# First half's input projection and convolution as one TensorE product, second half's softplus and B/C parts off VectorE, the memsets ahead of them

## The reference, cut to what matters

```
x  = einsum('ed,bld->bel', in_proj_w, hidden)         # input projection
xc = conv over l, 4 taps per channel, causal          # xp padded by 3
u  = silu(xc + conv_b)
dt_lo, B, C = split(einsum('ke,bel->bkl', x_proj_w, u))   # 8, 16, 16 rows
delta = softplus(einsum('er,brl->bel', dt_proj_w, dt_lo) + dt_proj_b)
A = -exp(A_log)
step: state = state * exp(delta * A) + (delta * u) * B ;  y = sum_n state * C
y = (y + D * u) * silu(z)                              # z: layer norm of x
```

## Time and profile before

| | us |
|---|---|
| median of 3 runs (lowest, highest) | 882.12 (879.97, 882.24) |
| the profiled execution, its own time | 880.29 |
| its span, first to last instruction | 878.5 |
| busy in the span: PE, DVE, ACT, POOL | 785.6, 572.9, 451.5, 424.5 |

### The profile page before, as it was taken

The page is one execution under the profiler, slowest core; times in us unless marked ns, Lnnn a source line. Parts: engine busy times, 40 slices in busy tenths (PEclk is TensorE's granted clock), DMA queues, the critical chain, the costliest instruction groups (busy, mean ns, idle before and its releaser), DMA issues. The chain is left out here.

```text
span 878.5 us, 13771 instructions
## 1 busy us (share of the span) xinstructions
PE 785.6 (89%) x4691; PEld 659.1 (75%) x4694; DVE 572.9 (65%) x948; ACT 451.5 (51%) x911; POOL 424.5 (48%) x325
## 2 busy tenths in 40 slices
PE   7366576699999996999999999999979999999997
PEld 2122222378888885999999999999858888888886
DVE  7999999845333345888888888888766433333333
ACT  4433344273343334777777777777634343433432
POOL 1464666136565645435344353443224565655653
PEclk9686999899999999999999999999979999999999
DMA  4321100101334302101010010000011443333341
GB/s 152 147 96 48 48 0 0 37 19 56 102 107 121 106 24 73 65 8 38 1 37 19 17 36 0 0 0 1 1 37 37 111 125 107 106 121 102 107 118 56
DMA packets 17665, 52.43 MB, mean 60 GB/s; under 512 B 2969, under 2 KB 5602, under 8 KB 16610
## 3 DMA queue, kind: packets, MB, share of 16 engines
q1 hardware_dynamic: 17360, 51.51, 18.8%
q10 hardware_dynamic: 274, 0.53, 0.2%
HBM read 50.83 MB, written 1.21 MB: 59 GB/s over the span
## 5 line engine op out<-in xcount | busy, mean ns | idle before, releaser
L953 DVE TENSOR_TENSOR f_su<-f_sg,psum 128x512 f32<-128x512 f32 x84 | 57.7, 687 | 199.5 <-PE psum L87 181.9
L850 POOL TENSOR_TENSOR f_h_lo<-f_hid,f_h_hi 128x512 fp32r<-128x512 f32 x84 | 108.7, 1295 | 117.2 <-ACT f_h_hi L836 112.3
L85 PE MATMUL psum<-xT_hi,f_gu_hi 128*128 128x512 f32 x336 | 133.0, 396 | 5.1 <-DVE xT_lo L587 3.2
L836 ACT ACTIVATE f_h_hi<-f_hid 128x512 fp32r<-128x512 f32 x84 | 53.1, 632 | 156.5 <-DVE f_hid L965 156.5
L86 PE MATMUL psum<-xT_lo,f_gu_hi 128*128 128x512 f32 x336 | 132.4, 394 | 0.0
L87 PE MATMUL psum<-xT_hi,f_gu_lo 128*128 128x512 f32 x336 | 131.4, 391 | 0.0
L371 POOL TENSOR_TENSOR m_dbu<-m_du,m_b_all 128x1024 f32<-128x1024 f32 x32 | 75.5, 2364 | 47.6 <-DVE m_hst L440 44.0
L85 PE MATMUL psum<-f_dn_hi,f_h_hi 128*128 128x256 f32 x336 | 94.9, 282 | 1.5 <-POOL f_h_lo L850 1.5
L87 PE MATMUL psum<-f_dn_hi,f_h_lo 128*128 128x256 f32 x336 | 95.1, 283 | 0.0
L86 PE MATMUL psum<-f_dn_lo,f_h_hi 128*128 128x256 f32 x336 | 95.0, 283 | 0.0
L1339 POOL TENSOR_TENSOR a_rr<-a_ss,eps 128x8 f32<-128x8 f32 x32 | 6.4, 200 | 160.0 <-DVE a_ss L1376 160.0
(11 more groups left out here) (188 smaller groups left out, 2114.0 us busy)
## 6 DMA issues: line engine op xcount, KB each, us to landing
f_raw<-in_moe SPq DMA_DIRECT2D x42, 384.0 KB, 3.0
m_b_all<-b_rows SPq DMA_DIRECT2D x8, 1024.0 KB, 4.9
...
```

The costliest lines, as they stand in the source:

```text
L85: pe.matmul(out, a[0], b[0], start=first, stop=False, skip_group_check=True)
L836: act.activation(h_hi[:, hs, :], hid[:, hs, :], ACT.Copy).then_inc(h_hi_s, 1)
L850: return pool.tensor_tensor(out, whole, hi, ALU.subtract)
L953: dve.tensor_tensor(su[:, hs, :], sg[:, hs, :], up_bank(half), ALU.mult).then_inc(su_s, 1)
```

## The change

The first half's projection and convolution become one operation on PE: the 4 x 256 taps are loaded as one row (`taps_row`), spread over the partitions by two products with a row of ones, and multiplied on DVE with w_in (`weighed_taps`) into four weight matrices a group. `convolved(g)` adds four shifted products in PSUM, and ACT reads the result there. The second half keeps projection and DVE taps; its two projections stand between `convolved(0)` and `convolved(1)`. ACT's silus are interleaved. In half 1, `w_part` goes to ACT (and with it 1 - w, `sp_a`), max(x, 0) too, t, r, delta and du go to POOL behind its dbu products 6, 8, 10 and 12, the two copies of `c_parts` to ACT (k=1) and its last subtraction to POOL (k=4). POOL's power of the norm goes behind dbu(2). On DVE four of the eight statistics, all sums and vare go behind the two memsets, which now follow `c_rest(1)`; nmr goes behind weighted(8). The arithmetic of the other parts is the same. Lines left out are marked by "...".

```diff
 w_in = sb("w_in", [P, DI])
+taps_row = sb("taps_row", [1, G * DC * P])
+ones = sb("ones", [1, P])
+w_tap = sb("w_tap", [P, G, DC, P])
 chan = sb("chan", [P, G, PC_N])
...
 sel = sb("sel", [3 * NBC, DS, P], BF16)
-conv = sb("conv", [P, 2, G, HALF])
+conv = sb("conv", [P, G, HALF])
 u = sb("u", [P, 2, G, HALF])
...
 sp_w = sb("sp_w", [P, 2, G * HALF])
+sp_a = sb("sp_a", [P, G * HALF])
 sp_r = sb("sp_r", [P, 2, G * HALF])
...
-chan_in, dt_in, ident_in, x_in, sel_in = (
-    sem(n) for n in ("chan_in", "dt_in", "ident_in", "x_in", "sel_in"))
+chan_in, dt_in, taps_in, x_in, sel_in = (
+    sem(n) for n in ("chan_in", "dt_in", "taps_in", "x_in", "sel_in"))
 ctx_in = [sem(f"ctx_in{h}") for h in range(2)]
...
 LN_VAR, LN_SHIFT = 2 * NT + 1, 2 * NT + 2
-PADS, DA_ZERO = 4, 6
+PADS, DA_ZERO = 5, 7
+XIN_BROADCAST, XIN_CONV, XIN_LATE = (1, 2), (3, 6), (4, 5)
+U = ((1, 3), (2, 4))
 da_ready, dbu_ready, scanned, c_psum, hc_ready, y_added = (
...
     def _(sp):
+        sp.dma_start(taps_row[:, :], d["taps"]).then_inc(taps_in, 16)
         sp.dma_start(w_in[:, :], d["w_in"]).then_inc(ctx_in[0], 16)
...
         sp.dma_start(sh.ctxT[:, HALF:T], d["ctxT"][:, HALF:T]).then_inc(ctx_in[1], 16)
-        sp.dma_start(ident[:, :], d["ident"]).then_inc(ident_in, 16)
+        sp.dma_start(ident[:, :], d["ident"]).then_inc(sel_in, 16)
         sp.dma_start(x[:, :, :], d["x"].rearrange("(t p) f -> p t f", p=P)).then_inc(x_in, 16)
...
         keep_warm(pe, sh, 7, 4)
-        for h in range(2):
-            pe.wait_ge(ctx_in[h], 32 if h == 0 else 16)
+        pe.wait_ge(pads, PADS)
+        pe.wait_ge(taps_in, 16)
+        for g in range(G):
+            pe.matmul(bank(6 + g), ones[:, :], taps_row[:, g * DC * P:(g + 1) * DC * P], start=True, stop=True)\
+                .then_inc(xin, 1)
+        def convolved(g):
+            pe.wait_ge(conv_step, g + 1)
+            src = sh.ctxT[:, 0:HALF].rearrange("p (b l) -> p b l", b=2)
+            dst = bank(g).rearrange("p (b l) -> p b l", b=2)
+            for late in range(DC):
+                mm = pe.matmul(dst[:, :, late:L], w_tap[:, g, DC - 1 - late, :], src[:, :, 0:L - late],
+                               start=(late == 0), stop=(late == DC - 1), skip_group_check=True)
+            mm.then_inc(xin, 1)
+        def project(h):
             for g in range(G):
-                pe.matmul(bank(2 * h + g), w_in[:, g * P:(g + 1) * P],
-                          sh.ctxT[:, h * HALF:(h + 1) * HALF], start=True, stop=True).then_inc(xin, 1)
-        def project(h):
-            for g in range(G):
-                pe.wait_ge(u_ready, G * h + g + 1)
+                pe.wait_ge(u_ready, U[h][g])
                 mm = pe.matmul(xz_bank(h)[0:3 * NBC + DR, :], chan[:, g, PC_XP:PC_N], u[:, h, g, :],
...
+        pe.wait_ge(ctx_in[0], 32)
+        convolved(0)
+        pe.wait_ge(ctx_in[1], 16)
+        for g in range(G):
+            pe.matmul(bank(2 + g), w_in[:, g * P:(g + 1) * P], sh.ctxT[:, HALF:T], start=True, stop=True)\
+                .then_inc(xin, 1)
+        convolved(1)
         pe.wait_ge(chan_in, 16)
...
         project(1)
-        pe.wait_ge(conv_step, DC * 2 * G)
         steps_in(1)
         pe.wait_ge(dg_ready, 1)
+        pe.wait_ge(conv_step, G + DC * G)
         skip(0)
-        pe.wait_ge(sel_in, 16)
+        pe.wait_ge(sel_in, 32)
         pe.wait_ge(bc_step, BC_ALL(0))
...
-        def gated(h):
-            for g in range(G):
-                act.wait_ge(conv_step, DC * (G * h + g + 1))
-                act.activation(u[:, h, g, :], conv[:, h, g, :], ACT.Silu, bias=chan[:, g, PC_CB:PC_CB + 1])\
-                    .then_inc(u_ready, 1)
+        def gated(h, g):
+            if h == 0:
+                act.wait_ge(xin, XIN_CONV[g])
+                v = bank(g)
+            else:
+                act.wait_ge(conv_step, G + DC * (g + 1))
+                v = conv[:, g, :]
+            act.activation(u[:, h, g, :], v, ACT.Silu, bias=chan[:, g, PC_CB:PC_CB + 1]).then_inc(u_ready, 1)
...
         act.wait_ge(chan_in, 16)
-        gated(0)
+        gated(0, 0)
+        gated(1, 0)
+        gated(0, 1)
         act.wait_ge(pads, PADS)
         low_rank(0)
+        gated(1, 1)
         b_and_c(0)
-        gated(1)
         act.preload_act_table_set("natural_log_exp_and_others")
...
             decays(k)
+            if k == 1:
+                act.wait_ge(bc_step, BC_R(1))
+                act.activation(bc3[NBC:2 * NBC, 1, :], bc_r[NBC:2 * NBC, 1, :], ACT.Copy)
+                act.activation(bc3[2 * NBC:3 * NBC, 1, :], bc_r[2 * NBC:3 * NBC, 1, :], ACT.Copy).then_inc(bc_step, 1)
             if k == 3:
...
                 act.activation(sp_e[:, 1, :], sp_e[:, 1, :], ACT.Exp, scale=-1.0).then_inc(sp_exp, 1)
+            if k == 4:
+                act.wait_ge(sp_exp, 2)
+                act.activation(sp_w[:, 1, :], sp_e[:, 1, :], ACT.Identity, bias=1.0).then_inc(delta_step, 1)
+                act.wait_ge(delta_step, SP_W(1))
+                act.activation(sp_a[:, :], sp_w[:, 1, :], ACT.Identity, scale=-1.0, bias=1.0).then_inc(sp_exp, 1)
+            if k == 5:
+                act.activation(sp_x[:, :], sp_x[:, :], ACT.Relu).then_inc(sp_abs, 1)
             if k == 6:
-                act.wait_ge(delta_step, SP_W(1))
                 act.activation(delta[:, 1, :, :], sp_w[:, 1, :].rearrange("p (g t) -> p g t", g=G), ACT.Ln)\
...
         pool.tensor_tensor(sh.c_lo[:, :], sh.ctxT[:, :], sh.c_hi[:, :], ALU.subtract)
-        pool.wait_ge(ln_step, LN_VAR)
-        pool.tensor_tensor(rstd[:, :], vare[:, :], sh.mhalf[:, 0:NT], ALU.pow).then_inc(ln_rstd, 1)
+        C_LOW = 4
+        def c_low(h):
+            pool.wait_ge(bc_step, BC_MID(h))
+            pool.wait_ge(dbu_ready, C_LOW + 1)
+            pool.tensor_tensor(bc3[2 * NBC:3 * NBC, h, :], bc_r[2 * NBC:3 * NBC, h, :], bc3[2 * NBC:3 * NBC, h, :],
+                               ALU.subtract).then_inc(bc_step, 1)
+            pool.wait_ge(bc_step, BC_ALL(h))
+        def t_part(h):
+            pool.wait_ge(sp_exp, 3)
+            pool.tensor_tensor(sp_e[:, h, :], sp_e[:, h, :], sp_a[:, :], ALU.add).then_inc(delta_step, 1)
+        def r_part(h):
+            pool.wait_ge(delta_step, SP_T(h))
+            pool.wait_ge(sp_abs, 3)
+            pool.tensor_tensor(sp_r[:, h, :], sp_x[:, :], sp_e[:, h, :], ALU.add).then_inc(delta_step, 1)
+        def delta_part(h):
+            pool.wait_ge(delta_step, SP_R(h))
+            pool.wait_ge(sp_ln, h + 1)
+            v = delta[:, h, :, :].rearrange("p g t -> p (g t)")
+            pool.tensor_tensor(v, v, sp_r[:, h, :], ALU.add).then_inc(delta_step, 1)
+        def du_part(h):
+            pool.wait_ge(delta_step, DELTA(h))
+            pool.wait_ge(u_ready, U[h][1])
+            pool.tensor_tensor(du[:, h, :, :], delta[:, h, :, :], u[:, h, :, :], ALU.mult).then_inc(delta_step, 1)
+        beside = {C_LOW: c_low, 6: t_part, 8: r_part, 10: delta_part, 12: du_part}
         for k in range(STEPS):
...
                                b_all[:, n:n + 1, :].to_broadcast([P, G, HALF]), ALU.mult).then_inc(dbu_ready, 1)
+            if k == 2:
+                pool.wait_ge(ln_step, LN_VAR)
+                pool.tensor_tensor(rstd[:, :], vare[:, :], sh.mhalf[:, 0:NT], ALU.pow).then_inc(ln_rstd, 1)
+            if k in beside:
+                beside[k](1)
         norm_deviation(pool, sh, after, 0)
...
         dve.memset(sh.eps[:, :], EPS).then_inc(pads, 1)
+        dve.memset(ones[:, :], 1.0).then_inc(pads, 1)
         dve.memset(dt_lo[:, :, :], 1.0).then_inc(pads, 1)
-        def taps(h):
+        def weighed_taps(g):
+            dve.wait_ge(xin, XIN_BROADCAST[g])
+            dve.tensor_tensor(w_tap[:, g, :, :], bank(6 + g).rearrange("p (j c) -> p j c", j=DC),
+                              w_in[:, g * P:(g + 1) * P].unsqueeze(1).to_broadcast([P, DC, P]), ALU.mult)\
+                .then_inc(conv_step, 1)
+        def taps():
             for g in range(G):
-                dve.wait_ge(xin, G * h + g + 1)
-                src = bank(2 * h + g).rearrange("p (b l) -> p b l", b=2)
-                out = conv[:, h, g, :].rearrange("p (b l) -> p b l", b=2)
+                dve.wait_ge(xin, XIN_LATE[g])
+                src = bank(2 + g).rearrange("p (b l) -> p b l", b=2)
+                out = conv[:, g, :].rearrange("p (b l) -> p b l", b=2)
                 for n, j in enumerate(reversed(range(DC))):
...
                     else:
-                        dve.wait_ge(conv_step, DC * (G * h + g) + n)
+                        dve.wait_ge(conv_step, G + DC * g + n)
                         dve.scalar_tensor_tensor(out[:, :, late:L], src[:, :, 0:L - late], w, out[:, :, late:L],
...
-        def c_parts(h):
+        def c_rest(h):
...
             dve.tensor_tensor(bc_r[:, h, :], xz_bank(h)[0:3 * NBC, :], bc_hi[:, h, :], ALU.subtract).then_inc(bc_step, 1)
+        def c_parts(h):
             dve.wait_ge(bc_step, BC_R(h))
...
             dve.wait_ge(bc_step, BC_MID(h))
-            dve.wait_ge(bc_hi_s, 2 * h + 2)
```

(37 more changed lines are left out.)

## The result

The changed kernel takes 869.90 us in the median of four runs (863.83 to 870.62), the kernel before 882.18 (879.97 to 882.59). The ratio is 0.985, with a 95% interval of 0.981 to 0.988: faster by 1.2 to 1.9%. The profiled executions are 880.29 and 863.83, so 16.5 us apart. Run again on another occasion, the changed kernel had a median of 865.85 against 882.12 (0.982, 0.979 to 0.985).

A forecast was written before the change was run, and what follows sets the result against it. VectorE, without idle time in the mixer loop, was taken as the bound. -5.3 + 0.5 - 13.9 + 1.2 + 0.3 = -17.2 us took 880.29 to 863.1; adding 0.9 gave a median of 864.0, range 860.3 to 869.5.

The forecast's parts named there:

- -5.3: Ahead of the loop: first scan at 35.0 instead of 40.26 us, 5.3 us earlier, ends -4.7 and -6.1.
- +0.5: Ahead of the first scan: vare on DVE held up while POOL is in dbu, between nothing and 1.9 us.
- like L412 in the loop: Case for vare: a DVE instruction with one SBUF input took 1.94 us where 0.68 was its time.
- 14.4 (13.1): Start: second-half taps on DVE begin at 14.4 (13.1) us and end at 20.4 (19.1).
- -13.9: Mixer loop: five second-half softplus instructions leave DVE and the 2.31 us wait goes too, 13.9 us saved.
- +1.2: Loop at k=8: nmr on DVE, expected to wait half a dbu beside busy POOL, costing 1.2 us.
- Rival (a): Loop up to dbu(13): POOL becomes the bound, +4 us, 868; chance 0.14.
- +0.3: Loop: POOL's products late for DVE's scans, nothing to +1.5 us, taken as 0.3.
- 0.17 plus a whole dbu: Loop: upper end for nmr, its own 0.17 us plus one whole POOL product of 2.35.
- (b): Start: PE stays at half speed throughout, giving +0.7 in place of -5.3, with 869 to 870 us; chance 0.08.
- (c): Loop and beyond: PE's clock stays low, slower, 878 us after the loop and up to 888; chance 0.04.
- (d): Loop: moved work is only waited for elsewhere, delta not ready at k=16, gain under 0.3%; chance 0.02.

The follow-up runs named there:

- vare_pool: Changed kernel with vare computed by GpSimd just ahead of its power, not by VectorE: 864.94 us, 0.982 of the kernel before.
- cparts_dve: Changed kernel with the three slow c_parts(1) instructions back on VectorE behind the memsets: 874.72 us, 0.990 of the kernel before.
- start_only: Kernel before with only the change's start on TensorE, everything behind it as before: 887.87 us, 1.006 of the kernel before.
- no_conv: Changed kernel without the start on TensorE, projection and all sixteen tap instructions as before: 862.69 us, 0.977 of the kernel before.
- best: no_conv with vare on GpSimd and nmr between scan(25) and weighted(24): 859.12 us, 0.975 of the kernel before.
- vare_nmr: vare_pool with nmr also moved from behind weighted(8) to between scan(25) and weighted(24): 862.36 us, 0.979 of the kernel before.
- softplus_only: Kernel before with only half 1's softplus moved off VectorE to ScalarE and GpSimd: 866.68 us, 0.981 of the kernel before.
- pool_extra: Changed kernel with two more 128x1024 GpSimd instructions, behind dbu(5) and dbu(7): 868.08 us, 0.981 of the kernel before.

## Why the prediction was right

**The sum.** It said 863.1 for the profiled execution and 864.0 for the median. The profiled execution is 863.83, the medians are 869.90 and 865.85. All lie in the range of 860.3 to 869.5 but the median of 869.90, which is 0.4 above it. The mechanism was that of the forecast. In the profile, -2.8 (first scan), -12.8 (scans 2 to 31) and -1.2 (all behind) make the -16.8.

**What was luck.** The mixer gave 15.6 us and not the 17.2 of the sum. The 1.2 behind it, where the sum had nothing and the same code varies by up to 7.9 us between profiles, brought the number close; and the profiled execution was the fastest of the six on record, the others taking 866.14 to 870.62. Against the median of 882.18 the change brought 12.3 us there and 16.3 us the second time, where 18.1 were forecast from 882.12. Both profiled executions of the changed kernel (863.83 and 864.84) were short ones, so where the 870 us executions lost their time is open.

**The start.** Expected -5.3 and for vare +0.5; measured -2.8. Of the 2.0 us missing from -4.8, about 1.5 are vare: the step "if it goes like L412 in the loop ... up to 1.9 us; if like the scans, nothing. I take +0.5" took a value near the wrong end. It went like L412: 2.13 us, 1.96 over its own time. vare_pool and cparts_dve show it by taking either the instruction or GpSimd's work away. The row to go by was the nearer one; it was even named. The rest of the start came as worked out, at its late end or up to 0.2 us past it: spreading products to 6.8 (6.79), taps to 19.1 to 20.4 (20.60), exponential to 25.5 to 27.0 (27.01), du at 31.2 to 32.7 (32.77). But two misses cancelled on the way. The products with the weighed taps began at 8.37 and not at 6.8, since ctxT was there at 7.5, 2.7 us later than the 4.80 of before and so beyond the 2 us that I had held to be harmless; VectorE idled 5.16 us for it. The weighing waits for ctxT although it reads only w_in and the taps (one semaphore counts both loads), and so its first multiplication (about 0.65 us) came behind the landing; no run has it wait for w_in alone. Against that, the eight pieces of convolved(0) took 5.16 us, where the first eight of before had taken 6.75, and ended at 13.53; the taps began at 14.50, where the late end had 14.4. Behind the -5.3, the 6.8 and the 14.4 (13.1) stands an estimate of the author's, a product of 1.7 us at half the clock (6.75 us for four) and of 0.9 at the full one, with the clock rising at 11 us at the earlier end; no run shows half the clock or a rise there. The granted clock reads 1.00 from 0 to 12 us in all fourteen profiles, and in the changed kernel the products took 1.89 us each (spreading), 1.29 (convolved(0)), 0.94 (the two projections) and 0.90 (convolved(1)).

**That this part costs.** "VectorE is relieved of half the taps and ends them no sooner" holds: 20.60 against 19.1, and start_only is slower than before. no_conv shows that without it the first scan comes 3.6 us earlier, best against vare_nmr 4.6. In the times of no_conv it can't be seen (862.69 and 865.85, overlapping intervals), and in its profile the long nmr cost 4.6 us more than in the changed kernel. best, which is without this part, without that wait and without vare on VectorE, is below the changed kernel.

**The loop.** -13.9 was exact (softplus_only: 96.06 us against 109.93). nmr +1.2 was 1.17 in the profile. ScalarE and GpSimd hid the moved work as reckoned; Identity and Relu took 1.04 to 1.06 us on ScalarE, with no table load at them. Rival (a) stayed away: at dbu(9) GpSimd's margin of 0.5 us (0.5 in vare_pool too, where it ended at 64.84 and scan 9 began at 65.33) grew by the 2 us that vare held VectorE, to the 2.5 that pool_extra measured. The +0.3 was nothing, and in vare_nmr, without vare's wait, 0.15 us at scan 13.

**A bound that was wrong, unseen.** For nmr the upper end was "0.17 plus a whole dbu". no_conv had 5.77 and pool_extra 8.12. In both profiles of the changed kernel nmr waited for one instruction (1.17 and 1.19). Whether a longer wait stands in those of its executions that took 870 us is not shown.

**The other rivals.** (b) did not come: a piece took 1.19 us at the start of convolved(0) and 0.59 at its end, 5.16 for eight, and convolved(1) took 3.58 for eight. Half speed in the first products, there and in the kernel before, was the author's estimate from such durations; the granted clock reads 1.00 from 4.8 to 11 us in the kernel before, where the first eight pieces took 6.75 us, and 1.00 from 3 to 18.6 us in the changed kernel. Why the first products are slow stays open. (c) did not: 100 to 140 us was granted 1.00. What it reckoned for a step with half the clock stands in before: the four pieces of additions took 3.62 us at 46.30, with 0.50 granted, and 1.88 at 52.87, with 1.00, and c_rows starts at 45.90 and again at 49.72, 3.82 apart. (d) did not: no scan waits at k=16.
